# Clamp and square root of the distances by pairs of heads instead of by whole groups of four

## The reference

```python
q, k, v = heads(xn @ Wq.T), heads(xn @ Wk.T), heads(xn @ Wv.T)
diff_sq = max(|q|^2 + |k|^2 - 2 q.k, 0)
denom = max((1 - |q|^2) * (1 - |k|^2), 1e-6)
cosh_arg = max(1 + 2 * diff_sq / denom, 1)
attn = softmax(-arccosh(cosh_arg))          # over the keys
out = x + (attn @ v) @ Wo.T + (xn @ int4(kernel) + bias + xn @ a @ b)
```

## Time and profile before

| | |
|---|---|
| median of three runs | 2607.86 us |
| the profiled execution | 2615.11 us |
| its span, first to last instruction | 2613.4 us |
| busy: TensorE, ScalarE, VectorE | 2318.2, 2159.3, 2086.7 us |
| mean granted TensorE clock | 0.975 of full speed |

### The profile page before, as it was taken

The page is one execution under the profiler, slowest core; times in us unless marked ns, Lnnn a source line. Parts: engine busy times, 40 slices in busy tenths (PEclk is TensorE's granted clock), DMA queues, the critical chain, the costliest instruction groups (busy, mean ns, idle before and its releaser), DMA issues. The chain is left out here.

```text
span 2613.4 us, 44986 instructions
## 1 busy us (share of the span) xinstructions
PE 2318.2 (89%) x17416; PEld 810.0 (31%) x17416; DVE 2086.7 (80%) x2780; ACT 2159.3 (83%) x2022; POOL 252.1 (10%) x75
## 2 busy tenths in 40 slices
PE   4889989999999999999999999999999999977774
PEld 1433333333333333333333333333333333321111
DVE  7778878888887888887888888888888887866663
ACT  2258898889888888988898888888889888999990
POOL 1011011101101110110111011011101101000000
PEclk8999999999999999999999999999999999999997
DMA  3542332444244343534524433443435344243314
GB/s 124 147 133 70 78 101 81 122 120 126 88 120 133 93 110 112 144 93 118 133 82 121 127 113 106 122 133 93 110 113 135 100 113 125 81 129 84 84 39 118
DMA packets 357001, 285.82 MB, mean 109 GB/s; under 512 B 81296, under 2 KB 296464, under 8 KB 356784
## 3 DMA queue, kind: packets, MB, share of 16 engines
q1 hardware_dynamic: 356784, 282.91, 39.3%
HBM read 160.30 MB, written 121.63 MB: 108 GB/s over the span
## 5 line engine op out<-in xcount | busy, mean ns | idle before, releaser
L416 ACT ACTIVATE root<-pU 128x1024 f32<-128x1024 f32 x1024 | 1016.0, 1027 | 31.5 <-PE pU L189 31.1
L420 ACT ACTIVATE root<-root 128x2048 f32<-128x2048 f32 x512 | 981.0, 1916 | 58.1 <-DVE root L653 56.2
L189 PE MATMUL pU<-QS,KS 100*128 100x512 f16 x2048 | 623.0, 387 | 175.9 <-ACT root L416 172.7
L653 DVE TENSOR_SCALAR root<-root 128x2048 f32<-128x2048 f32 x512 | 627.7, 1226 | 82.1 <-ACT root L416 78.8
L658 DVE TENSOR_TENSOR root<-root 128x2048 f32<-128x2048 f32 x256 | 584.5, 2283 | 14.9 <-ACT root L420 13.7
L199 PE MATMUL pO<-root,VX 128*32 128x512 f32 x4096 | 556.0, 613 | 2.3 <-ACT root L420 2.3
L767 POOL TENSOR_TENSOR xt<-xt,bias_b 128x512 f32<-128x512 f32 x64 | 243.3, 3803 | 1908.3 <-DVE xn L552 1901.6
L189 PEld LDWEIGHTS pU<-QS,KS 100*128 100x128 f16 x2048 | 139.6, 98 | 727.8 <-ACT root L416 387.3
L213 PE MATMUL pZ<-root,ones 128*32 128x512 f32 x2048 | 276.7, 611 | 1.0 <-DVE root L658 1.0
L565 DVE TENSOR_REDUCE nrm<-sqr 128x16 f32<-128x512 f32 x128 | 87.5, 683 | 144.7 <-ACT sqr L445 144.7
L257 PE MATMUL pM<-Wvh,xT 128*128 128x512 f16 x512 | 181.5, 399 | 2.6 <-ACT qk L441 2.6
(11 more groups left out here) (106 smaller groups left out, 2253.2 us busy)
## 6 DMA issues: line engine op xcount, KB each, us to landing
v_d<-v_o SPq DMA_DIRECT2D x64, 264.0 KB, 2.1
k_d<-kx SPq DMA_DIRECT2D x64, 264.0 KB, 2.1
KT<-k_d SPq DMA_DIRECT2D x64, 264.0 KB
VX<-v_d SPq DMA_DIRECT2D x64, 264.0 KB
xt<-in_x SPq DMA_DIRECT2D x32, 512.0 KB, 4.6
res_d<-f_o SPq DMA_DIRECT2D x64, 256.0 KB, 2.1
QS<-qh_d SPq DMA_DIRECT2D x128, 128.0 KB
KS<-kh_d SPq DMA_DIRECT2D x128, 128.0 KB
```

What stands on the lines that cost most here:

```text
L189: mm = pe.matmul(pU[:, col:col + HALF], KS[i][:, h, j * P:(j + 1) * P], QS[i][:, h, half * HALF:(half + 1) * HALF], start=True, stop=True)
L416: act.activation(root[:, q % RING, cols], pU[:, cols], ACT.Square).then_inc(squared, 1)
L420: act.activation(root[:, q % RING, :], root[:, q % RING, :], ACT.Sqrt).then_inc(rooted, 1)
L653: v.tensor_scalar(root[:, q % RING, :], root[:, q % RING, :], CS * CS, CS * CS, ALU.max, ALU.subtract).then_inc(clamped, 1)
```

## The change

Clamp and square root are given a pair t of 128 x 1024 values in place of a quad q of 128 x 2048. VectorE clamps pair s - 1 in every step, ScalarE takes the root of pair s - 2 in every step. The two readers of finished roots, `sum_v` and `add_pair`, wait for twice the count. No loop, buffer or ring length changes, and the number of values is the same; there are 1024 clamps and 1024 roots in place of 512 each.

```diff
--- before.py
+++ after.py
@@ -192,7 +192,7 @@
 
             def sum_v(q):
                 p, j = q // JC, q % JC
-                pe.wait_ge(rooted, q + 1)
+                pe.wait_ge(rooted, 2 * q + 2)
                 if j == 0 and p:
                     pe.wait_ge(o_taken, p)
                 for h in range(G4):
@@ -415,9 +415,10 @@
                     act.wait_ge(summed_up, q - RING + 1)
                 act.activation(root[:, q % RING, cols], pU[:, cols], ACT.Square).then_inc(squared, 1)
 
-            def sinh(q):
-                act.wait_ge(clamped, q + 1)
-                act.activation(root[:, q % RING, :], root[:, q % RING, :], ACT.Sqrt).then_inc(rooted, 1)
+            def sinh(t):
+                q, cols = t // 2, slice(t % 2 * 2 * HALF, (t % 2 + 1) * 2 * HALF)
+                act.wait_ge(clamped, t + 1)
+                act.activation(root[:, q % RING, cols], root[:, q % RING, cols], ACT.Sqrt).then_inc(rooted, 1)
 
             def take_v_sums(p):
                 act.wait_ge(v_summed, (p + 1) * JC)
@@ -484,8 +485,8 @@
                     take_one_sums(p - 1)
                 if s < 2 * QUADS:
                     square(s)
-                if s % 2 and 0 <= (s - 3) // 2 < QUADS:
-                    sinh((s - 3) // 2)
+                if 0 <= s - 2 < 2 * QUADS:
+                    sinh(s - 2)
                 if p < PERIODS:
                     behind(p, k)
 
@@ -648,12 +649,13 @@
                 t = res_i[:, o % 2, :]
                 v.scalar_tensor_tensor(out=t, in0=pM[b][:, :], scalar=scale[:, IVO:IVO + 1], in1=t, op0=ALU.mult, op1=ALU.add).then_inc(taken["o"], 1)
 
-            def clamp(q):
-                v.wait_ge(squared, 2 * q + 2)
-                v.tensor_scalar(root[:, q % RING, :], root[:, q % RING, :], CS * CS, CS * CS, ALU.max, ALU.subtract).then_inc(clamped, 1)
+            def clamp(t):
+                q, cols = t // 2, slice(t % 2 * 2 * HALF, (t % 2 + 1) * 2 * HALF)
+                v.wait_ge(squared, t + 1)
+                v.tensor_scalar(root[:, q % RING, cols], root[:, q % RING, cols], CS * CS, CS * CS, ALU.max, ALU.subtract).then_inc(clamped, 1)
 
             def add_pair(q):
-                v.wait_ge(rooted, q + 1)
+                v.wait_ge(rooted, 2 * q + 2)
                 v.wait_ge(v_summed, q)
                 v.tensor_tensor(root[:, (q - 1) % RING, :], root[:, (q - 1) % RING, :], root[:, q % RING, :], ALU.add).then_inc(pair_added, 1)
 
@@ -743,8 +745,8 @@
                     moments((n + 3) // 2)
             for s in range(16 * PERIODS + 8):
                 p, k = s // 16, s % 16
-                if s % 2 == 0 and 0 <= s // 2 - 1 < QUADS:
-                    clamp(s // 2 - 1)
+                if 0 <= s - 1 < 2 * QUADS:
+                    clamp(s - 1)
                 if p < PERIODS:
                     behind(p, k)
                 if s % 4 == 3 and 0 <= (s - 5) // 2 < QUADS:
```

## The result

Four runs of the changed kernel take 2632.7 to 2634.2 us, median 2632.89; the kernel before has 2608.57 over four. The ratio is 1.0093, with a 95% interval of 1.0075 to 1.0110. From one profiled execution to the other the span grows by 18.0 us.

A forecast was written before the change was run, and what follows sets the result against it. No engine was taken as full; a loop of waits bounds the kernel. TensorE's terms sum to +0.6 us a pair, 17 us over 28 pairs; with the tail +19 on 2615.11, so 2634, median 2627; forecast range 2613 to 2642.

The forecast's parts named there:

- qk, +0.94 twice: Copy qk at k = 4, both periods: a half root ahead of it delays it and all later steps by 0.94 us.
- k = 0, -0.3: Even period, k = 0: TensorE's 0.58 us wait for a square shrinks by 0.3 us (between 0 and 0.58).
- k = 1, -0.8: Even period, k = 1: a half root replaces a whole one between squares, so TensorE's 0.81 us wait goes entirely.
- sqr, -0.1: ScalarE's sqr at k = 2, where SyncE's chain passes: it starts about 0.1 us earlier.
- VectorE from norm to aug rows, -0.3: VectorE's stretch from norm to augmented rows: five half clamps (3.10 us) replace three whole ones (3.39), 0.3 us less.
- SyncE's chain: Path through sqr, VectorE's norm to augmented rows and SyncE's KV copies; forecast to grow +0.5 us to a pair.
- k = 13, -0.15: Even period, k = 13: TensorE's 0.89 us wait for a square shrinks by 0.15 us.
- the sum of +0.6 to a pair: TensorE's stream from one KV wait to the next, all terms added: +0.6 us per pair of periods, 17 us over 28.
- the clock rival: The new wait at k = 5 falls in the half-clock stretch behind the KV wait: +31 us, 2658; chance 0.11.
- The last 8 periods, +2 us: Periods without qk, ScalarE alone binding: 64 quads x 0.08 = 5 us more, of which idleness takes back some 3.
- The price of a piece: Start-to-start cost: half root 0.94 us on ScalarE (bounds 0.90 and 1.01), half clamp 0.62 on VectorE (0.57 to 0.70).

The follow-up runs named there:

- after_kv_first: The changed kernel with SyncE issuing the KV copies ahead of the stack loads, which move from k = 9 to k = 12; 2571.4 us, ratio 0.985.
- qk4_first: The changed kernel with the copy qk and the square of the keys ahead of the half root again at k = 4; 2585.8 us, ratio 0.991.
- before_late_qk: The kernel before with only the root due at k = 5 cut, its first half at k = 4 between square and copy qk; 2658.8 us, ratio 1.0173.

## Why the prediction was right, and where its terms were off

The direction, the median (2627 against 2632.9) and the cause held: a half root in front of qk costs more than the pairs give back elsewhere. The terms, each by its number in the forecast:

1. *qk, +0.94 twice.* Its start moved by 0.95; the visible wait is 0.92, or 0.46 to 0.49 in 11 of the 18 odd periods that wait for KV, and 48.3 us in all. Shown by taking it out and by adding it alone.
2. *k = 0, -0.3.* Mis-sized: nothing. Averaged over the even periods 10 to 52 of the timeline TensorE waits 0.60 us before and 0.57 after. ln still waits 1.22 us for VectorE (1.31 before), so the half root ahead of it does not fill ScalarE's idle time, and the moments are not early enough.
3. *k = 1, -0.8.* Held: the 0.81 is gone.
4. *sqr, -0.1.* Wrong in sign: from the start of "ln" to that of "sqr" it was 8.06 us and is 8.25 (1235.54 to 1243.79). The overhead of four half roots is there, the earlier start is not.
5. *VectorE from norm to aug rows, -0.3.* Held: 18.2 us before, 17.8 after, without a wait between, so -0.4. Points 4 and 5 together give -0.2 in place of -0.4, and SyncE's chain kept step with TensorE: 18 waits for KV, 34.6 and 35.2 us.
6. *k = 13, -0.15.* Mis-sized in the other direction: 0.89 to 0.33, so -0.56.

Without KV's wait, the sum of +0.6 to a pair is measured at +0.70. With it the 48 periods grew by 28.8 / 24 = 1.2 to a pair. The other half goes with the clock rival: the new wait falls in the stretch behind the wait for KV, and the number of odd periods with half clock went from 10 to 15. It was a rival with 0.11, but it does not exclude the forecast; it adds to it. That it stands behind the KV wait is shown by after_kv_first, where the odd periods have no such stretch though every wait for qk is there.

TensorE's busy and idle time separate the two. The matmuls are the same, so more busy time is slower work. In the 48 periods the change adds 26.7 us of busy and 2.1 of idle time; with the KV copies first it adds 5.9 (1686.13 to 1692.06) and 11.0. So the forecast's sum of waits, 0.6 to a pair, shows mostly as waits without the slow clock (11.0 / 24 = 0.46). With it TensorE is late itself and its waits shrink, as that for qk does in the 11 odd periods named above. The late copy has both parts, as the same periods of qk4_first show, and behind them those of before_late_qk:

```profile
454.14:2264.67 1810.53, 1704.44 (x13053) 600.46 (x13053) 1551.78 (x2419) 1635.01 (x1895) 136.68 (x46) 0.99 0.42 115
...
459.27:2332.29 1873.02, 1719.89 (x13053) 603.60 (x13053) 1526.73 (x2034) 1616.14 (x1559) 189.03 (x46) 0.98 0.41 111
```

Against the changed kernel the first is 28.5 us less of busy and 20.8 less of idle time; against the kernel before the second is 13.7 more of busy and 28.3 more of idle time. So between a third and somewhat over half of the late copy's price is slower work, which the forecast's own sum had at nothing. No run holds the clock fixed, so this divides the time and is not a test of its own.

*The last 8 periods, +2 us.* Wrong in sign: 8.0 us less. ScalarE was not full there. In seven periods it was busy for 211.66 of 224.79 us before and is for 215.16 of 216.78 after: the finer steps fill its idle time, and the dips of TensorE's clock nearly vanish (0.95 to 0.99). The other traces repeat it: these seven periods take 222 to 226 us in all six kernels that take the root of a quad at one place, and 215 to 218 in all six with half roots spread over the steps (before_late_qk, which spreads one of eight, has 220). The window I had read, 31.19 of 32, was one of the fuller ones. This is 10 us less than forecast, and it offsets most of the clock's addition.

*The price of a piece.* The half root takes 0.95 from start to start (0.94 taken). The half clamp takes 0.60 (0.62 taken), as one and then two in a row on VectorE's timeline after show, 1.29 less 0.69:

```profile
1188.54 0.69 DVE L655 TENSOR_SCALAR root<-root 128x1024 f32<-128x1024 f32 x1
...
1189.54 1.29 DVE L655 TENSOR_SCALAR root<-root 128x1024 f32<-128x1024 f32 x2
```

The total came close in part by luck: a clock that cost more than forecast, a k = 0 that gave nothing, a k = 13 that gave 0.4 more and a tail that shrank instead of growing nearly cancel.

## What to carry to other kernels

When a long instruction is cut and spread over steps, look at each short instruction that somebody waits for and that used to run before it: the piece that moves ahead of it delays the waiter by its full length. Put such copies first and the pieces behind them; here that order was worth 47 us, while the finer grain itself gave 25. Look also at what a new wait stands behind: following a wait of 2 us on the matrix engine it cost clock as well, and with that first wait gone the same change cost 10 us in place of 24. The order of DMAs that removed it was worth 50 us to the kernel before, twice what the change cost.

## What the runs showed of the hardware

GpSimd's addition of the bias, which nobody touched, became faster with the clamp by pairs: 3.8 us on average with half clamps back to back, 2.4 after the change. The two groups:

```profile
L768 POOL TENSOR_TENSOR xt<-xt,bias_b 128x512 f32<-128x512 f32 x64 | 242.3, 3787 | 1919.8 <-DVE xn L552 1913.2 <-issue 6.7
```

```profile
L769 POOL TENSOR_TENSOR xt<-xt,bias_b 128x512 f32<-128x512 f32 x64 | 152.0, 2375 | 2024.6 <-DVE xn L553 2017.6 <-issue 6.9
```

It is not the shorter clamp that does it, since back to back the halves change nothing. The means mix short and long ones, here of an odd and of an even period after the change, with VectorE's clamp of the newest pair in the odd one:

```profile
1216.13 1.26 POOL L769 TENSOR_TENSOR xt<-xt,bias_b 128x512 f32<-128x512 f32 x1 [34.49 <-DVE xn L553]
1256.76 4.48 POOL L769 TENSOR_TENSOR xt<-xt,bias_b 128x512 f32<-128x512 f32 x1 [39.37 <-DVE xn L553]
...
1217.99 0.69 DVE L655 TENSOR_SCALAR root<-root 128x1024 f32<-128x1024 f32 x1 [1.94 <-ACT root L416]
```

In the odd period that clamp waits for its square, so VectorE is idle for 1.94 us behind "xn", and the addition takes 1.26 us in that gap. In the even period VectorE works on behind "xn" without a pause, and it takes 4.48. Before the change the addition of two quads follows "xn" in both, and 54 of the 64 bias additions take over 3.2 us; after it 22 do. This is read from traces; no run changed it by itself.

With the KV copies first, the clock showed no half rate in any odd period between 8 and 55, though in after_kv_first TensorE waits 0.6 and 0.9 us in close succession in each. Three of its even periods do hold such a stretch, at the same two waits. In this one TensorE waits 0.63 us at 1141.17 and 0.92 at 1142.70:

```profile
1142.00:1147.00 5.00, 4.30 (x18) 1.16 (x22) 4.83 (x10) 3.13 (x5) 0.00 (x0) 0.66 0.01 3
```

So the two short waits alone go with half clock in 3 of these 48 periods, and after the change, in the odd periods with a wait for KV, in 15 of 18; before it, without the wait for qk, it is 10 of 18.
